# Per-head projections as float32 in column halves, and the second head's turned rows copied by two engines

## The chip, the cores and the metric

The kernel runs on one core of a Trainium2 chip. The time is the device time of one execution in microseconds (us). Every number of the trace comes from one profiled execution on that core. The engines are named as the profile names them: PE is TensorE (PEld its weight loads), DVE is VectorE, ACT is ScalarE, POOL is GpSimd, SP issues most of the DMAs.

## The reference, cut to what matters

The program is a network of two layers on x of 2 batches of 1024 rows of 128. Layer 0 is one causal attention head and a mixture of experts. Layer 1, in which nearly all of the time goes, is attention with 16 heads of 64 columns and a bias by relative position, and then a feed-forward part with 8 low-rank experts.

```python
h = _layernorm(x) * (1 + ca) + sa
q, k, v = shape(h @ Wq), shape(h @ Wk), shape(h @ Wv)      # 16 heads of 64
scores = einsum('bhqd,bhkd->bhqk', q, k)
weights = softmax(scores + position_bias)
context = einsum('bhqk,bhkd->bhqd', weights, v)
x = x + ga * (context.reshape(B, S, H * Dk) @ Wo)
```

The products that the change touches are h @ Wq, h @ Wk and h @ Wv of this layer.

## The kernel before, in words

Heads go in 8 pairs, and a pair and a batch make a unit: 16 units (UNITS). A unit has 8 tiles of 128 query rows, so there are 128 tiles (TILES), and the attention is one software pipeline of slots n, one tile per slot. All engines run the slots in the same order, each in its own function, and semaphores tie them; no scheduler moves anything, so the order of the code is the order on the engine.

In slot n PE runs `pe_slot`: the scores of tile n+2 (`pe_scores`: three passes of high and low parts in fp32r, two heads in row halves of the array, 12 matmuls of 512 columns into the banks SC), the turning of head 0's weights of tile n (`pe_turn`: 16 transposes into the two banks PT[0] and PT[1]), one chunk of the next unit's projections into the bank MI where the slot has one (`pe_chunk`), half of the weights-times-values product of the tile pair before (`pe_values`, the heads in column halves of the array, into CX), the turning of head 1 into the same two banks PT, and, in even slots, the product with Wo (`pe_wo`).

A unit has six chunks: q and k in two halves each of 512 columns, v in two halves of four row tiles. They stand in slots 0, 1, 2, 3, 5 and 7 of the unit before. So every odd slot holds a chunk, and slots 4 and 6 hold none. The last unit has no chunks to make, and unit 0's chunks are made before the slots begin. A q or k chunk is three fp32r matmuls of 128 x 128 weights against 512 columns: high h by high w, low h by high w, high h by low w. For this ACT writes `h_high` behind each `hT`, DVE or POOL writes `h_low`, and POOL writes `wsplit` (`pool_split`) for every head pair. A v chunk is four float32 matmuls of 128 columns.

The two banks PT are one buffer for both heads. Head 0's turned rows are copied by ACT (`act_turned`), head 1's by DVE (`dve_turned`), each 1024 columns out of both banks. `pe_turn(n, 1)` waits for ACT's copy of the same slot (`ptA_out`), and `pe_turn(n, 0)` for DVE's copy of the slot before (`ptB_out`).

In slot n ACT runs, in this order: head 0's copy, the exponential of tile n+2's head 0, the chunk's copy out of MI, the exponential of head 1, and in odd slots the copy of the context (`ctxs`). DVE runs, in this order: in odd slots the two products out of `pe_wo` (`dve_wo`), the bias and row maximum of tile n+2 for both heads (`dve_biased`), and head 1's copy.

Before the slots, a quarter of the rows at a time is gathered from the experts, normalised (`norm_scaled` on DVE), turned on PE (`turn_rows`, line 1160) and written to `hT` by ACT (line 753). The last two quarters, batch 1, come between slots 0 and 1.

Of the kernel before, what the change touches and what calls it, by code (L numbers as in the profile page):

```python
# [14 lines left out]
F32 = mybir.dt.float32  # L15
# [7 lines left out]
P = 128  # L23
# [41 lines left out]
def build(nc, rel_hot, L0_attn_x, L0_attn_Wq, L0_attn_bq, L0_attn_Wk, L0_attn_bk, L0_attn_Wv, L0_attn_bv,  # L65
# [4 lines left out]
    with ExitStack() as ctx:  # L70
# [18 lines left out]
        h_high = sb("h_high", [P, N], F32R)  # L89
        h_low = sb("h_low", [P, N], F32R)  # L90
        h_parts = (h_high, h_low)
# [25 lines left out]
        wsplit = sb("wsplit", [P, 2, 2, 2, P], F32R)  # L117
# [39 lines left out]
        lowrank = [part(h_high, 0, 512), part(h_high, 512, 512)]  # L157
        masked = h_low[:, :].rearrange("p (j a n) -> p j a n", j=2, a=2)
# [123 lines left out]
        def act_chunk(act, u, c):  # L282

            kind, q = chunk_of(u, c)
            act.wait_ge(ev("proj_full"), 6 * u + c + 1)
# [41 lines left out]
        def pe_chunk(pe, u, c):  # L327
# [3 lines left out]
            if c == 0 and b == 0:  # L331
                pe.wait_ge(ev("w_split"), p + 1)
# [5 lines left out]
            else:  # L338
                n = (u - 1) * TB + slots_of(u)[c]
                if u == 1 and c == 0:  # L340
                    pe.wait_ge(ev("low_out"), 4)
# [35 lines left out]
        def pe_turn(pe, n, hd):  # L377
# [17 lines left out]
        def pe_values(pe, g, half):  # L395

            if half == 0:
                pe.wait_ge(ev("ptA_out"), 2 * g + 2)
                pe.wait_ge(ev("ptB_out"), 2 * g + 2)
                pe.wait_ge(ev("ctx_out"), g)  # L400
# [74 lines left out]

        def act_exp(act, n, hd):
# [8 lines left out]
        def act_slot(act, n):  # L485
# [11 lines left out]
            if n + 2 < TILES:  # L497
                act_exp(act, n + 2, 1)
            if n >= 3 and n % 2 == 1:
# [19 lines left out]
        def dve_turned(dve, n):  # L519
# [4 lines left out]
            dve.tensor_copy(turned_out(n, 1), turned_in(1)).then_inc(ev("ptB_out"), 1)  # L524
# [37 lines left out]
        def pool_split(pool, p):  # L562

# [837 lines left out]
```

## Time and profile before

| | us |
|---|---|
| median of 3 runs | 1039.62 (1037.82 to 1041.65) |
| the profiled execution's own time | 1039.06 |
| its span, first to last instruction | 1037.3 |
| PE busy | 934.1 (90%) |
| DVE busy | 668.4 (64%) |
| ACT busy | 590.0 (57%) |
| POOL busy | 281.7 (27%) |

The profiled execution lies 1.8 us over its span and 0.6 us under the median. The slots run from about 224 us to 946 us of the span. In front of them stand layer 0 and the gathering of the experts' rows, behind them the last feed-forward part. A timeline row gives the start, the length from the first start to the last end of a merged group, the engine, the line, what is written from what, and the number of instructions. A float32 matmul of the program is two matmul instructions in the trace, each with its weight load. The length of a matmul reaches beyond the start of the next, since they are pipelined, so the distance between the starts of two groups tells what a group takes from PE.

### The profile page before, as it was taken

The page shows a single profiled execution, that of the slowest core. Times are in us where ns is not written, and L with a number is a line of the kernel's source. Part 1 is how long each engine was busy: PE and PEld are TensorE (multiplying, and loading weights), DVE is VectorE, ACT ScalarE, POOL GpSimd, SP SyncE. Part 2 cuts the span into 40 slices and gives each one's busy share as a digit, 9 for nine tenths or more (in the row PEclk, how much of TensorE's full clock was granted, in tenths as well). Part 3 has the DMA queues.
Part 4 walks back from the last instruction along what each step waited for, and adds up shares of the span by engine and source line. Part 5 has one row for each costly group of instructions (what it writes and reads, how often), then busy time and mean ns, then how long its engine had stood idle before and what let it go on. Part 6 is the DMA issues. An engine that isn't in the chain of part 4 may idle for free. (4 is left out here: it accounts for less than half of the span.)

```text
span 1037.3 us, 24542 instructions
## 1 busy us (share of the span) xinstructions
PE 934.1 (90%) x9958; PEld 687.5 (66%) x9958; DVE 668.4 (64%) x1352; ACT 590.0 (57%) x980; POOL 281.7 (27%) x332
## 2 busy tenths in 40 slices
PE   7888349457999999999999999999999999996897
PEld 6467338345777777677777767777777776774786
DVE  6277401285767777677677777667777776774665
ACT  2533113236666766766766676676667667672343
POOL 1100540332341422324233142333414233112300
PEclk9999769767999999999999999999999999999999
DMA  8301231100002002000200200110020010000000
GB/s 260 109 1 73 94 89 31 56 23 1 2 2 85 2 2 86 2 2 2 85 3 1 86 2 2 42 46 3 2 85 2 2 37 3 1 3 2 1 21 21
DMA packets 27124, 35.43 MB, mean 34 GB/s; under 512 B 6042, under 2 KB 21716, under 8 KB 26836
## 3 DMA queue, kind: packets, MB, share of 16 engines
q1 hardware_dynamic: 25988, 31.76, 9.2%
q0 software_dynamic: 1024, 2.10, 0.7%
q8 instruction: 80, 1.31, 0.5%
q14 instruction: 32, 0.26, 0.1%
HBM read 28.48 MB, written 5.37 MB: 33 GB/s over the span
## 5 line engine op out<-in xcount | busy, mean ns | idle before, releaser
L516 DVE CUSTOM_DVE_ANT_0 soft<-SC,strips 128x1024 f32<-128x1024 f32 x256 | 303.2, 1221 | 21.1 <-PE SC L372 21.1
L482 ACT ACTIVATE soft<-soft,nmax 128x1024 f32<-128x1024 f32 x256 | 294.0, 1149 | 2.8 <-DVE nmax L516 2.8
L524 DVE COPY PTs<-PT 128x1024 f32<-128x1024 f32 x128 | 156.8, 1225 | 186.0 <-PE PT L390 186.0
L474 ACT COPY PTs<-PT 128x1024 f32<-128x1024 f32 x128 | 129.8, 1014 | 223.9 <-PE PT L390 223.9
L406 PE MATMUL CX<-PTs,V 128*64 128x256 f32 x2048 | 250.7, 387 | 5.7 <-DVE wo_out L533 4.3
L372 PE MATMUL SC<-qk 64*128 64x512 f32 x1536 | 212.4, 409 | 10.4 <-DVE nmax L516 7.0
L390 PEld LDWEIGHTS PT<-ident,soft 64*128 64x128 f32 x4096 | 155.6, 139 | 86.5 <-issue 75.6
L406 PEld LDWEIGHTS CX<-PTs,V 128*64 128x64 f32 x2048 | 136.7, 137 | 89.7 <-issue 24.6
L390 PE MATMUL PT<-ident,soft 64*128 64x64 f32 x4096 | 180.1, 228 | 3.7 <-DVE PTs L524 2.4
L372 PEld LDWEIGHTS SC<-qk 64*128 64x128 f32 x1536 | 137.1, 188 | 35.5 <-issue 4.7
L557 POOL TENSOR_TENSOR x<-x,wo_out 128x256 f32<-128x256 f32 x64 | 47.1, 736 | 259.3 <-DVE wo_out L533 259.3
L322 POOL CAST qk<-raw_qk 128x512 fp32r<-128x512 f32 x60 | 36.8, 614 | 225.1 <-ACT raw_qk L298 225.1
L324 POOL TENSOR_TENSOR qk<-raw_qk,qk 128x512 fp32r<-128x512 f32 x60 | 77.5, 1292 | 4.8
L354 PE MATMUL MI<-h_high,wsplit 128*128 128x512 f32 x122 | 55.6, 455 | 2.9 <-DVE h_low L1045 2.9
L482 ACT ACTIVATION_READ_ACCUMULATOR soft<-soft,nmax 128x1 f32 x256 | 49.3, 193 | 0.0
L806 ACT ACTIVATE probsT<-SC,cols 128x384 f32<-128x384 f32 x32 | 18.6, 581 | 53.9 <-PE SC L1280 52.4
L560 POOL TENSOR_TENSOR x<-x,wo_out 128x256 f32<-128x256 f32 x64 | 47.5, 742 | 5.0
L425 PE MATMUL CX<-wog,ctxs 64*128 64x128 f32 x256 | 42.4, 286 | 0.5 <-ACT ctxs L505 0.5
L425 PE MATMUL MI<-wog,ctxs 64*128 64x128 f32 x256 | 42.4, 286 | 0.0
L1130 PE MATMUL SC<-ident 128*128 128x128 f32 x110 | 17.4, 316 | 24.9 <-DMA slots_in<-probsT,arena 24.9
L841 ACT ACTIVATE probsT<-SC,cols 128x512 f32<-128x512 f32 x32 | 21.9, 690 | 28.2 <-PE SC L1363 28.1
L298 ACT ACTIVATE raw_qk<-MI 128x512 f32<-128x512 f32 x60 | 35.2, 587 | 0.0
(235 smaller groups left out, 1041.4 us busy)
## 6 DMA issues: line engine op xcount, KB each, us to landing
strips<-bias_vec SPq DMA_DIRECT2D x8, 1920.0 KB, 7.1
arena<-in_L_ffn_w SPq DMA_DIRECT2D x1, 2048.0 KB, 10.4
slots_in<-arena SPq DMA_DIRECT2D x1, 1536.0 KB, 9.1
arena<-slots_in SPq DMA_DIRECT2D x8, 192.0 KB, 3.9
slots_out<-arena SPq DMA_DIRECT2D x8, 192.0 KB, 2.0
x<-in_L_attn_x SPq DMA_DIRECT2D x2, 512.0 KB, 4.6
out<-x SPq DMA_DIRECT2D x4, 256.0 KB, 2.3
arena<-in_L_wmod SPq DMA_DIRECT2D x2, 384.0 KB, 5.6
```

The lines of the kernel that those rows point to most:

```text
L324: pool.tensor_tensor(qk[u % 2][:, k + 1, at], raw_qk[:, c % 2, :], qk[u % 2][:, k, at].bitcast(F32), ALU.subtract).then_inc(ev("low_out"), 1)
L354: ins = pe.matmul(bank, wsplit[:, p % 2, wp, "qk".index(kind), :], rhs, start=(n == 0), stop=(n == 2))
L372: ins = pe.matmul(SC[hd][:, k * CK:(k + 1) * CK], qk[u % 2][mine, qp, i * P:(i + 1) * P], qk[u % 2][mine, kp, k * CK:(k + 1) * CK], start= ...
L390: ins = pe.transpose(PT[r][:, t * DK:(t + 1) * DK], soft[mine, n % RING, hd, t * P:(t + 1) * P], ident[mine, mine])
L406: ins = pe.matmul(CX[hd * DK:(hd + 1) * DK, 0:2 * P], V1[:, vb, t, hd * DK:(hd + 1) * DK], PTs[:, g % 2, hd, t, :], start=(t == 0), stop=( ...
L425: ins = pe.matmul(dst, ctxs[mine, g % 4, t * P:(t + 1) * P], wog[mine, u % B, u // B, :], start=(hd == 1 or (g == GROUPS - 1 and t == 0)), ...
L474: act.copy(turned_out(n, 0), turned_in(0)).then_inc(ev("ptA_out"), 1)
L482: act.activation(soft[:, n % RING, hd, :], soft[:, n % RING, hd, :], ACT.Exp, bias=nmax[:, j:j + 1], scale=-1.0, accum_out=rsum[:, hd, n % ...
L516: dve.tensor_tensor_reduce(soft[:, n % RING, hd, :], SC[hd][:, :], strips[:, u // B % 2, hd, i * P:i * P + S], 1.0, 3.4e38, ALU.add, ALU.m ...
L524: dve.tensor_copy(turned_out(n, 1), turned_in(1)).then_inc(ev("ptB_out"), 1)
L557: pool.tensor_tensor(x[:, t0:t0 + 2, :], x[:, t0:t0 + 2, :], wo_out[:, g % 2, 1, :, :], ALU.add).then_inc(ev("x_half"), 1)
L560: pool.tensor_tensor(x[:, t0:t0 + 2, :], x[:, t0:t0 + 2, :], wo_out[:, g % 2, 0, :, :], ALU.add).then_inc(ev("x_added"), 1)
```

## The change

1. A q or k chunk is now two float32 matmuls, one for each head of the pair: the weights are 64 columns of `wpair`, the output the partitions 0 to 63 or 64 to 127 of the bank, the moving operand the 512 columns of `hT` for both. A v chunk is eight float32 matmuls, two for each row tile: 64 columns of `hT` as weights, `wpair` (128 columns) moving.
2. `h_high`, `h_low` and `wsplit`, with all instructions that write them, are gone. PE waits for `hT_ready` and `ld_pair` in their place.
3. Head 1's turned rows are copied in two parts: DVE takes PT[0], ACT takes PT[1] (`act_turned_half`), 512 columns each. ACT does its part behind the exponential of head 1 and ahead of the copy of the context. `pe_turn(n, 0)` and `pe_values` wait for both.
4. On DVE slot -1 comes ahead of the scaling of batch 1's rows (`norm_rows(2, (1,))`), which stood between slots -2 and -1.
5. `proj_full` counts two for each chunk, and the buffers `lowrank` and `masked` of the last part are buffers of their own.

```diff
@@ pe_chunk
-            if kind == "v":
-                for t in range(4):
-                    ins = pe.matmul(bank[:, t * P:(t + 1) * P], hT[:, b * S + (4 * q + t) * P:b * S + (4 * q + t + 1) * P], wpair[:, p % 2, 2, :], start=True, stop=True)
-            else:
-
-                for n, (hp, wp) in enumerate(((0, 0), (1, 0), (0, 1))):
-                    rhs = h_parts[hp][:, b * S + q * CK:b * S + (q + 1) * CK]
-                    if kind == "q":
-                        rhs = bass.AP(h_parts[hp], b * S + S - 1 - q * CK, [[N, P], [-1, CK]])
-                    ins = pe.matmul(bank, wsplit[:, p % 2, wp, "qk".index(kind), :], rhs, start=(n == 0), stop=(n == 2))
-            ins.then_inc(ev("proj_full"), 1)
+            rhs = hT[:, b * S + q * CK:b * S + (q + 1) * CK]
+            if kind == "q":
+                rhs = bass.AP(hT, b * S + S - 1 - q * CK, [[N, P], [-1, CK]])
+            for t in range(4 if kind == "v" else 1):
+                for r in range(2):
+                    mine = slice(r * DK, (r + 1) * DK)
+                    if kind == "v":
+                        at = b * S + (4 * q + t) * P + r * DK
+                        ins = pe.matmul(bank[mine, t * P:(t + 1) * P], hT[:, at:at + DK], wpair[:, p % 2, 2, :], start=True, stop=True)
+                    else:
+                        ins = pe.matmul(bank[mine, :], wpair[:, p % 2, "qk".index(kind), mine], rhs, start=True, stop=True)
+                    if t == 3 or kind != "v":
+                        ins.then_inc(ev("proj_full"), 1)
@@ pe_turn, head 0 (and the same wait in pe_values)
                     pe.wait_ge(ev("ptB_out"), n)
+                    pe.wait_ge(ev("ptB_half"), n)
@@ new, called in act_slot behind the second act_exp
+        def act_turned_half(act, n):
+
+            act.wait_ge(ev("ptB_full"), 2 * n + 2)
+            if n >= 4:
+                act.wait_ge(ev("pv_done"), n // 2 - 1)
+            act.copy(turned_out(n, 1)[:, 1, :, :], PT[1][:, :].rearrange("p (t q) -> p t q", t=TB)).then_inc(ev("ptB_half"), 1)
@@ dve_turned
-            dve.tensor_copy(turned_out(n, 1), turned_in(1)).then_inc(ev("ptB_out"), 1)
+            dve.tensor_copy(turned_out(n, 1)[:, 0, :, :], PT[0][:, :].rearrange("p (t q) -> p t q", t=TB)).then_inc(ev("ptB_out"), 1)
@@ norm_out on ACT (the subtraction into h_low goes on DVE and POOL, too)
-                    if n == 2:
-
-                        act.wait_ge(ev("hT_ready"), 4 * n + k + 1)
-                        at = slice(reversed_block(k) * 512, (reversed_block(k) + 1) * 512)
-                        act.copy(h_high[:, at], hT[:, at]).then_inc(ev("h_high"), 1)
@@ vector
             dve_slot(dve, -2)
+            dve_slot(dve, -1)
             norm_rows(2, (1,))
-            for n in range(-1, TILES + 4):
+            for n in range(TILES + 4):
@@ tensor
-            pe.wait_ge(ev("h_split"), 1)
+            pe.wait_ge(ev("hT_ready"), 9)
...
-            pe.wait_ge(ev("h_split"), 4)
```

On PE, in an odd slot and the start of the even one behind it, there stood before (L354 is the chunk, L406 the values, L390 the transposes, L372 the scores):

```order
L354 MATMUL MI<-h_high,wsplit 128x512
L406 MATMUL CX<-PTs,V 64x256 [waits s_woA_out]
L406 MATMUL CX<-PTs,V 64x256 x7
L390 MATMUL PT<-ident,soft 128x64 [waits s_ptA_out,s_exp_done]
L390 MATMUL PT<-ident,soft 128x64 x15
L372 MATMUL SC<-qk 128x512 [waits s_nmax_done]
L372 MATMUL SC<-qk 128x512 x11
L390 MATMUL PT<-ident,soft 128x64 [waits s_ptB_out,s_exp_done]
L390 MATMUL PT<-ident,soft 128x64 x15
L354 MATMUL MI<-h_high,wsplit 128x512 [waits s_woB_out,s_high_out]
L354 MATMUL MI<-h_low,wsplit 128x512
L354 MATMUL MI<-h_high,wsplit 128x512
```

In the changed kernel the same place reads (L352 is the chunk, L407 the values, L371 the scores):

```order
L352 MATMUL MI<-hT,wpair 64x512
L407 MATMUL CX<-PTs,V 64x256 [waits s_woA_out]
L407 MATMUL CX<-PTs,V 64x256 x7
L390 MATMUL PT<-ident,soft 128x64 [waits s_ptA_out,s_exp_done]
L390 MATMUL PT<-ident,soft 128x64 x15
L371 MATMUL SC<-qk 128x512 [waits s_nmax_done]
L371 MATMUL SC<-qk 128x512 x11
L390 MATMUL PT<-ident,soft 128x64 [waits s_ptB_half,s_ptB_out,s_exp_done]
L390 MATMUL PT<-ident,soft 128x64 x15
L352 MATMUL MI<-hT,wpair 64x512 [waits s_woB_out,s_high_out]
L352 MATMUL MI<-hT,wpair 64x512
```

The order of the groups is the same. The chunk writes 64 partitions at a time, as the values behind it do, and the first transposes of the even slot wait for one semaphore more.

On ACT, the end of an odd slot and the start of the next, before (L482 is the exponential, L505 the context, L474 head 0's copy, L298 the chunk):

```order
L298 ACTIVATE raw_qk<-MI 128x512 [waits s_low_out,s_proj_full]
L482 ACTIVATE soft,rsum<-soft,nmax 128x1024 [waits s_rinv_done,s_nmax_done]
L505 COPY ctxs<-CX 128x256 [waits s_woB_full,s_woA_full,s_pv_done]
L474 COPY PTs<-PT 128x2x8x64 [waits s_pv_done,s_ptA_full]
L482 ACTIVATE soft,rsum<-soft,nmax 128x1024 [waits s_rinv_done,s_nmax_done]
```

And in the changed kernel (L490 is the exponential, L482 now the new half copy, L515 the context, L285 a v chunk, L475 head 0's copy):

```order
L285 COPY V1<-MI 128x512 [waits s_pv_done,s_proj_full]
L490 ACTIVATE soft,rsum<-soft,nmax 128x1024 [waits s_rinv_done,s_nmax_done]
L482 COPY PTs<-PT 128x8x64 [waits s_pv_done,s_ptB_full]
L515 COPY ctxs<-CX 128x256 [waits s_woB_full,s_woA_full,s_pv_done]
L475 COPY PTs<-PT 128x2x8x64 [waits s_pv_done,s_ptA_full]
```

One copy more stands behind the second exponential, ahead of the context's copy.

On DVE, at the first slots, before (L516 is the bias and maximum, L884 to L890 the scaling of batch 1's rows):

```order
L516 ISA soft,nmax<-SC,strips 128x1024 [waits s_strips0,s_scores]
L516 ISA nmax 128x1
L884 RECIPROCAL st<-st 128x8 [waits s_root_ready,s_var_ready]
L885 TENSOR_TENSOR st<-st 128x8 [waits s_dve_step]
...
L890 TENSOR_SCALAR probs<-x,mv,st 128x128 x7
L516 ISA soft,nmax<-SC,strips 128x1024 [waits s_scores]
L516 ISA nmax 128x1
```

And in the changed kernel (L526 is the bias and maximum, L873 to L879 the scaling):

```order
L526 ISA soft,nmax<-SC,strips 128x1024 [waits s_scores]
L526 ISA nmax 128x1
L526 ISA soft,nmax<-SC,strips 128x1024 [waits s_scores]
L526 ISA nmax 128x1
L873 RECIPROCAL st<-st 128x8 [waits s_root_ready,s_var_ready]
L874 TENSOR_TENSOR st<-st 128x8 [waits s_dve_step]
```

The bias and maximum of tile 1, which waits for that tile's scores, has moved ahead of the scaling.

## Rows read from the trace of the kernel before

**Rows 1.** The page: span, PE's busy time, PE's granted clock in 40 slices.

```profile
span 1037.3 us, 24542 instructions
PE 934.1 (90%) x9958; PEld 687.5 (66%) x9958; DVE 668.4 (64%) x1352; ACT 590.0 (57%) x980; POOL 281.7 (27%) x332
PEclk9999769767999999999999999999999999999999
```

**Rows 2.** The timeline, 500 to 512 us: an odd slot, then an even one.

```profile
500.57 1.23 PEld L372 LDWEIGHTS SC<-qk 64*128 64x128 f32 x12
501.84 0.74 PEld L390 LDWEIGHTS PT<-ident,soft 64*128 64x128 f32 x16
502.65 0.97 PEld L347 LDWEIGHTS MI<-wpair,hT 128*128 128x128 f32 x8
502.79 1.01 ACT L474 COPY PTs<-PT 128x1024 f32<-128x1024 f32 x1 [1.65 <-PE PT L390]
503.74 1.49 PEld L406 LDWEIGHTS CX<-PTs,V 128*64 128x64 f32 x16
505.31 1.16 ACT L482 ACTIVATE soft<-soft,nmax 128x1024 f32<-128x1024 f32 x1
505.62 0.58 PEld L390 LDWEIGHTS PT<-ident,soft 64*128 64x128 f32 x16 [0.39 <-issue]
506.11 1.24 PEld L372 LDWEIGHTS SC<-qk 64*128 64x128 f32 x12
506.40 1.23 DVE L524 COPY PTs<-PT 128x1024 f32<-128x1024 f32 x1 [1.76 <-PE PT L390]
506.46 0.37 ACT L505 COPY ctxs<-CX 128x256 f32<-128x256 f32 x1
507.75 0.61 PEld L390 LDWEIGHTS PT<-ident,soft 64*128 64x128 f32 x16 [0.40 <-issue]
508.42 0.19 PEld L354 LDWEIGHTS MI<-h_high,wsplit 128*128 128x128 f32 x1
508.53 1.02 ACT L474 COPY PTs<-PT 128x1024 f32<-128x1024 f32 x1 [1.71 <-PE PT L390]
509.32 1.49 PEld L406 LDWEIGHTS CX<-PTs,V 128*64 128x64 f32 x16 [0.37 <-issue]
```

**Rows 3.** The timeline, the first us of the values, asked in short windows.

```profile
509.32 0.44 PE L406 MATMUL CX<-PTs,V 128*64 128x256 f32 x2
509.32 0.14 PEld L406 LDWEIGHTS CX<-PTs,V 128*64 128x64 f32 x2 [0.37 <-issue]
509.59 0.82 PE L406 MATMUL CX<-PTs,V 128*64 128x256 f32 x6
```

**Rows 4.** Groups by line and shape: copies of 512 columns out of a bank.

```profile
L941 DVE COPY probsT<-PT 128x512 f32<-128x512 f32 x1 | 0.7, 692 | 0.9 <-PE PT L1214 0.9
L289 ACT COPY V<-MI 128x512 f32<-128x512 f32 x28 | 16.1, 575 | 0.0
```

**Rows 5.** The timeline by engine, 209 to 247 us: hT, its parts, PE behind them.

```profile
210.17 0.78 ACT L753 ACTIVATE hT<-SC,modc 128x512 f32<-128x512 f32 x1 [3.51 <-PE SC L1160]
212.98 0.80 PE L354 MATMUL PT<-h_high,wsplit 128*128 128x512 f32 x1 [2.84 <-DVE h_low L1045]
217.88 0.78 ACT L753 ACTIVATE hT<-SC,modc 128x512 f32<-128x512 f32 x1
220.72 0.80 PE L354 MATMUL MI<-h_high,wsplit 128*128 128x512 f32 x1 [2.92 <-DVE h_low L1045]
222.17 0.63 PE L354 MATMUL PT<-h_high,wsplit 128*128 128x512 f32 x1
222.59 0.63 PE L354 MATMUL PT<-h_low,wsplit 128*128 128x512 f32 x1
231.89 2.14 DVE L890 TENSOR_SCALAR probs<-x,mv,st 128x128 f32<-128x128 f32 x8
```

**Rows 6.** The same view: where PE waits for the last of h_low.

```profile
246.93 2.93 PE L372 MATMUL SC<-qk 64*128 64x512 f32 x12 [3.33 <-POOL h_low L710]
```

More of the change, by code:

```diff
@@ L88, in build @@
         x = sb("x", [P, NT, D])
-        h_high = sb("h_high", [P, N], F32R)
-        h_low = sb("h_low", [P, N], F32R)
-        h_parts = (h_high, h_low)
+        masked = sb("masked", [P, 2, 2, 512], F32R)
         with nc.sbuf_tensor("arena", [P, 8 * N], F32) as arena:
@@ L116, in build @@
         wpair = sb("wpair", [P, 2, 3, P])
-        wsplit = sb("wsplit", [P, 2, 2, 2, P], F32R)
+        lowrank = sb("lowrank", [P, 2, 512], F32R)
         strips = sb("strips", [P, 2, 2, STRIP])
@@ L284, in act_chunk @@
             kind, q = chunk_of(u, c)
-            act.wait_ge(ev("proj_full"), 6 * u + c + 1)
+            act.wait_ge(ev("proj_full"), 2 * (6 * u + c + 1))
             if kind == "v":
@@ L331, in pe_chunk @@
             if c == 0 and b == 0:
-                pe.wait_ge(ev("w_split"), p + 1)
+                pe.wait_ge(ev("ld_pair"), 48 * p + 48)
+            if c == 0 and u == 1:
+                pe.wait_ge(ev("hT_ready"), 12)
+                pe.wait_ge(ev("low_out"), 4)
             bank = chunk_bank(u, c)
@@ L399, in pe_values @@
                 pe.wait_ge(ev("ptB_out"), 2 * g + 2)
+                pe.wait_ge(ev("ptB_half"), 2 * g + 2)
                 pe.wait_ge(ev("ctx_out"), g)
@@ L498, in act_slot @@
                 act_exp(act, n + 2, 1)
+            if 0 <= n < TILES:
+                act_turned_half(act, n)
             if n >= 3 and n % 2 == 1:
@@ L575, in pool_slot @@
                 pool_chunk(pool, a, c)
-            if n % (B * TB) == 4 and n // (B * TB) + 1 < PAIRS:
-                pool_split(pool, n // (B * TB) + 1)
         block = ctx.enter_context(nc.Block())
@@ L631, in _ @@
                 if p >= 2:
-                    sp.wait_ge(ev("proj_full"), 12 * (p - 1))
+                    sp.wait_ge(ev("proj_full"), 24 * (p - 1))
                 load_weights(sp, p)
@@ L705, in _ @@
                                         bass.IndirectOffsetOnAxis(ap=slot_g[:, t:t + 1], axis=0)).then_inc(ev("gathered%d" % (t // 4)), 16)
-            for k in range(2, 4):
-                pool.wait_ge(ev("h_high"), k + 1)
-                at = slice(reversed_block(k) * 512, (reversed_block(k) + 1) * 512)
-                pool.tensor_tensor(h_low[:, at], hT[:, at], h_high[:, at].bitcast(F32), ALU.subtract).then_inc(ev("h_split"), 1)
             for n in range(-2, TILES + 4):
@@ L755, in norm_out @@
                                    bias=modc[:, layer, m, k // 2:k // 2 + 1]).then_inc(ev("hT_ready"), 1)
-                    if n == 2:
-                        act.wait_ge(ev("hT_ready"), 4 * n + k + 1)
-                        at = slice(reversed_block(k) * 512, (reversed_block(k) + 1) * 512)
-                        act.copy(h_high[:, at], hT[:, at]).then_inc(ev("h_high"), 1)
             norm_roots(0)
@@ L833, in _ @@
                     act.wait_ge(ev("masked"), 2 * k)
-                act.copy(lowrank[0], MI[:, :]).then_inc(ev("low_ready"), 1)
+                act.copy(lowrank[:, 0, :], MI[:, :]).then_inc(ev("low_ready"), 1)
                 for j in range(2):
@@ L1039, in quarter_rows @@
                 norm_scaled(quarter(q))
-            def split_h(k):
-                at = slice(reversed_block(k) * 512, (reversed_block(k) + 1) * 512)
-                dve.wait_ge(ev("h_high"), k + 1)
-                tt(h_low[:, at], hT[:, at], h_high[:, at].bitcast(F32), ALU.subtract).then_inc(ev("h_split"), 1)
             gathered(0)
@@ L1300, in _ @@
             turn_rows(2, 1)
-            pe.wait_ge(ev("h_split"), 2)
+            pe.wait_ge(ev("hT_ready"), 10)
             pe_chunk(pe, 0, 3)
```

19 lines of the change are left out of this document (3 added, 16 removed).

## The prediction

> **What bounds the kernel now.** I read the page first: PE is busy 90% of a span of 1037.3 us, and its granted clock is at the full level, 2.4 GHz, in every slice of the slots [rows 1]. So the 128 slots are PE's, and what counts is how far apart the starts of its groups lie. The timeline of one odd and one even slot shows that [rows 2]. The reader is to look at the distance between weight loads of successive groups on PEld. From the scores at 500.57 to the transposes at 501.84 it is 1.27 us, that is 12 matmuls in 6 pairs of row halves, 0.21 us for 512 columns in one pass. From the scores at 506.11 to the transposes at 507.75 it is 1.64 us for the same work. The difference is a wait: DVE's copy of head 1's turned rows starts at 506.40, takes 1.23 and ends at 507.63, and PE goes on 0.12 us later. At 501.84 there was no wait, since the product with Wo stood in between. The next group begins 0.81 us behind the unhindered transposes (502.65 - 501.84) and 0.67 us behind the delayed ones (508.42 - 507.75), since there the first weights are loaded while the scores still stream. Scores and transposes together take 2.08 us without the wait and 2.31 with it: the wait costs 0.23 us, not 0.37. It stands at the start of every even slot.
>
> The second thing to see is what a chunk takes: 0.90 us for q or k (508.42 to 509.32), of which three passes of 512 columns stream for 3 x 0.21 = 0.64, and 1.09 us for v (502.65 to 503.74). The values behind take 1.88 us (503.74 to 505.62), of which 8 pairs of column halves stream 1.71. A chunk thus carries about 0.25 us that is no streaming, and PEld is idle 0.37 us ahead of the values behind it [rows 2].
>
> **The waits of the even slots.** Split copies of 512 columns: DVE's costs 0.69 us and ACT's 0.58 us, both from rows of copies of that size out of a bank [rows 4]; DVE's price was 1.23 for 1024. DVE would end at 506.40 + 0.69 = 507.09. ACT has to end its exponential first (505.31 + 1.16 = 506.47), so it ends at 507.05, and with 0.12 for the release PE may go on at 507.17 to 507.21. PE is through with the scores at 506.11 + 1.27 = 507.38. The wait is gone, with 0.2 us to spare. If PE comes 0.23 us earlier because of a cheaper v chunk (below), ACT's half is as late as PE, at most 0.06 us later, and such a delay is paid by the load of the first weights, as the 0.81 against 0.67 shows. Odd slots have the Wo product in between (about 0.45 us more), so nothing waits there. ACT's added 0.58 us stands in idle time: it is idle 1.71 us ahead of the next copy at 508.53, behind the context's copy (506.46 + 0.37) [rows 2]. Queued behind the new copy are the context's copy, which PE's Wo product needs only a slot later, and head 0's copy, still over 1 us away. Were that cover gone, each of the 128 slots could cost up to 0.58. Even slots 2 to 124 have scores ahead of the transposes: 62 x 0.23 = 14.3 us. Behind them come two slots and the last values without scores to hide any of the copy. There the shorter copy shows by 1.23 - 0.69 = 0.5 us each: 1.5 us. **Term 1: -15.8 us.** What is late next is PE itself.
>
> **The chunks.** A float32 product streams twice the columns in each of its two instructions. The values show it: 256 columns, 8 products of each head half, and the starts of the pairs lie 0.21 us apart, since six matmuls that begin at 509.59 span 0.82 us, and a last one takes 0.38 to 0.44 of that [rows 3]. The two halves start together (two matmuls span 0.44 us, two loads 0.14) [rows 3], and 8 x 0.21 = 1.71 leaves no room for a stagger in the 1.88. So a new q or k chunk has 2 pairs of 512 columns, 2 x 0.43 = 0.85 us, and a new v chunk 8 pairs of 128 columns, 8 x 0.107 = 0.85 us. As to what is no streaming, the chunk now has the form of the values, 128*64, and runs into them: I take one start (0.06: 509.32 to 509.59 less 0.21) and one end for both, so that chunk and values take 0.85 + 1.88 = 2.73 us. Before it was 0.90 + 1.88 = 2.78 and 1.09 + 1.88 = 2.97. That is -0.04 for q and k, and -0.24 for v. There are 15 units with 4 and 2 of them in the slots: 60 x -0.04 + 30 x -0.24 = -9.6. The nearest bound on the other side is that the 0.24 remains at the border of chunk and values: q and k +0.19, v 0.0, in sum +11.4. I take the first end, because in the rows a border is paid where the form of the matmuls changes (0.17 us of the 1.88 behind the values) and groups of one form follow without loss (1.27 us for six pairs). **Term 2: -9.6 us.**
>
> The Trainium skill (TensorEngine Tiling, Key Properties) says that a change of the tiling mode drains TensorE. The PEld idle of 0.37 us between chunk and values agrees with it. Without that rule the sum would have +11.4 in place of -9.6.
>
> **The start.** PE waited for h_low. The first h was written at 210.17 + 0.78 = 210.95 and PE began at 212.98; the second at 218.66, and PE began at 220.72 [rows 5]. Each gives 2.0 us. In this stretch PE runs at the lower level, 1.2 GHz: the starts of 512-column passes lie 0.42 apart (222.17, 222.59). A q or k chunk of float32 is there 1.71 us against 1.28, +0.43, for four of them 1.7. Net -2.3. Later PE waits 3.33 us at 246.93 for POOL's h_low [rows 6], which goes whole: next is the turning of batch 1's rows, that ends at this wait's start. Against this stands the moved scaling on DVE. Its 8 instructions of 2.14 us and five small ones, about 3.1 us together, ran while PE made the scores of tile 1; now they come behind that tile's maximum and delay the next. I count that as +0.5, because the scores of tile 2 can meanwhile run; the bounds are 0 and +3.1. **Term 3: -2.3 - 3.3 + 0.5 = -5.1 us** (-2.5 to -7.5; the clock may also rise a little sooner).
>
> POOL loses 1.1 us for each head pair and was never waited for in the slots; the separate buffers at the end change no instruction. Both count nothing.
>
> **The sum.** 1039.06 - 15.8 - 9.6 - 5.1 = 1008.6 us, for the profiled execution; the median lies 0.6 higher, so 1009 us.
>
> **The rivals.** (a) *The wait stays*, because ACT's half comes late. ACT's chain in an odd slot is copy, exponential, chunk, exponential, half copy, from 502.79 to 507.05 without a hole, and PE's from 502.65 to 507.15 in the new kernel. The slack is thin, which speaks for it; that a delay under 0.14 us costs nothing speaks against. If it all stayed, term 1 falls to 1.5: 1023 us.
> (b) *The border stays*: chunk and values don't run together. 1009 + 21 = 1030 us. (a) and (b) together: 1044 us.
> (c) *Weights lie open.* Should loads of one column half not run beside matmuls of the other, each pair of loads adds its 0.14 us: 2 in a q or k chunk, 8 in a v chunk, 60 x 0.28 + 30 x 1.12 = +50, so 1059 us. The values speak against: with it their 8 pairs would take 2.8 us, and they take 1.88 [rows 2, 3]. The Trainium skill (TensorE: Matmul & The Clock Gate, Part 3) gives such a rule: weight loads overlap running matmuls only where the row group differs, and column halves share theirs. The trace does not agree with it here.
> (d) *The halves run one after another*, the slower end. Both halves of a q or k chunk read the same 512 columns, and write one bank. The values write one bank too, but read different data, so only this differs. Each chunk would stream 0.85 us more: 90 x 0.85 = +77, 1086 us. The change is slower than the kernel before from the point where a chunk costs 0.33 us more than I take (30 / 90).
> (e) *More than forecast*: the clock rises earlier at the start, and the last slots gain more: below 1001 us.
>
> **How the numbers follow.** Forecast 0.64, (a) 0.10, (b) 0.07, (a) and (b) 0.05, (c) 0.03, (d) 0.05, (e) 0.06. The bounds of terms 1 to 3 give the forecast 1002 to 1017. To hold 8 in 10 I go over (a), up to 1027, and down to 1001. A measurement of this kernel can tell 0.5%, about 5 us. Only (c) and (d) are slower than 1045, 0.08; (a) and (b) together give no change, 0.05; all else is faster, 0.87.
>
> **What would show it.** Right: the distance from scores to transposes is 1.27 us in even slots too; a q or k chunk begins 0.85 us ahead of its values, a v chunk as well; the idle of PEld ahead of the values is gone; an even and an odd slot with q and v chunks lie nearer by 0.5 us together; PE's first scores of tile 3 come at about 241.8, not 246.93. Wrong on term 1: transposes that start 0.1 us behind ACT's half copy, with the 1.27 not reached. Wrong on term 2: chunk to values 1.0 us or more, or pairs of the chunk whose starts lie 0.4 us apart within a pair. Wrong on term 3: a long idle of PE ahead of tile 2's scores or of the turning of batch 1's rows.

## The result and the profile after

The changed kernel takes 1010.09 us (median of 6 runs, 1007.98 to 1014.62), beside 1039.67 us (1037.82 to 1042.87) for the kernel before. The ratio is 0.9718, with an interval of 0.9691 to 0.9745. It is faster, and lies 1 us above the forecast of 1009. The profiled execution took 1007.98 us, over a span of 1006.1 us. From here on, "after" is the changed kernel.

The first lines of its page answer to [rows 1]. ACT and PE's clock stand with them, and so do the groups of the two half copies:

```profile
span 1006.1 us, 25473 instructions
PE 910.8 (91%) x10278; PEld 674.7 (67%) x10278; DVE 601.5 (60%) x1350; ACT 648.6 (64%) x1104; POOL 268.3 (27%) x314
PEclk9999769978999999999999999999999999997999
...
L534 DVE COPY PTs<-PT 128x512 f32<-128x512 f32 x128 | 88.5, 692 | 165.2 <-PE PT L390 165.1
L390 PE MATMUL PT<-ident,soft 64*128 64x64 f32 x4096 | 176.2, 226 | 3.7 <-ACT PTs L482 2.1
L482 ACT COPY PTs<-PT 128x512 f32<-128x512 f32 x128 | 74.0, 578 | 3.1 <-PE PT L390 3.1
```

The reader is to see that PE still bounds the kernel (91%), that DVE has 67 us less work and ACT 59 us more, and that the two copies cost 692 and 578 ns each, the prices of [rows 4]. The row of the transposes can't tell whether the wait of the even slots is gone. It puts 2.1 us to ACT's half (L482), in the whole execution, and the same row of the kernel before put 2.4 us to DVE's copy, where 62 waits of 0.23 us stood:

```profile
L390 PE MATMUL PT<-ident,soft 64*128 64x64 f32 x4096 | 180.1, 228 | 3.7 <-DVE PTs L524 2.4
```

The distances between the starts of groups do tell it.

The timeline of an odd slot and the start of the even one behind it answers to [rows 2]. L350 is a v chunk, L352 a q or k chunk, L407 the values, L390 the transposes, L371 the scores, L490 the exponential:

```profile
484.08 0.85 PEld L350 LDWEIGHTS MI<-wpair,hT 128*64 128x64 f32 x16
484.90 1.55 PEld L407 LDWEIGHTS CX<-PTs,V 128*64 128x64 f32 x16
486.74 1.16 ACT L490 ACTIVATE soft<-soft,nmax 128x1024 f32<-128x1024 f32 x1
486.83 0.57 PEld L390 LDWEIGHTS PT<-ident,soft 64*128 64x128 f32 x16 [0.39 <-issue]
487.32 1.24 PEld L371 LDWEIGHTS SC<-qk 64*128 64x128 f32 x12
487.61 0.69 DVE L534 COPY PTs<-PT 128x512 f32<-128x512 f32 x1 [1.54 <-PE PT L390]
487.88 0.58 ACT L482 COPY PTs<-PT 128x512 f32<-128x512 f32 x1
488.60 0.75 PEld L390 LDWEIGHTS PT<-ident,soft 64*128 64x128 f32 x16
489.42 0.20 PEld L352 LDWEIGHTS MI<-hT,wpair 128*64 128x64 f32 x4
489.90 0.15 PEld L407 LDWEIGHTS CX<-PTs,V 128*64 128x64 f32 x2 [0.28 <-issue]
490.33 1.44 PEld L407 LDWEIGHTS CX<-PTs,V 128*64 128x64 f32 x14 [0.28 <-issue]
```

From scores to transposes it is now 488.60 - 487.32 = 1.28 us in an even slot, where it was 1.64. DVE's half ends at 488.30 and ACT's at 488.46, and PE goes on at 488.60, 0.14 behind the later one. In the trace of before the transposes followed DVE's copy by 0.12. So ACT is just in time, with next to nothing to spare.

The v chunk begins 0.82 us ahead of its values, and chunk and values together take 2.75 (484.08 to 486.83). For a q or k chunk the same sum is 2.74 on the mean. But here the values load their first weights 0.48 behind the chunk's start, not 0.85: the two loads (x2 at 489.90) run while the chunk still streams, and then PEld is idle 0.28 until the values' matmuls begin at 490.33, 0.91 behind the chunk's first.

**Where the 31.2 us of span went.** I cut both executions at three marks: the first turning of gathered rows on PE, the first values and the last values.

| stretch | before | after | difference |
|---|---|---|---|
| up to the first turning | 209.05 | 206.78 | -2.3 |
| first turning to first values | 46.55 | 38.31 | -8.2 |
| first to last values (the slots) | 695.7 | 673.1 | -22.6 |
| last values to the end | 86.0 | 87.9 | +1.9 |

Of these the slots are the steadiest. Another execution of the same program (e7_after_again) gave 672.8, and so did two variants (e5, which leaves the slots alone, and e9, which moves one copy in them to another engine). The first stretch scatters: 206.5 to 211.9 in the twelve traces of this case.

The slots by their parts, as the mean distance between the starts of weight loads over some 55 places each, 30 for v:

| | before | after |
|---|---|---|
| even slot: scores to transposes, to the next group | 1.637 + 0.675 | 1.285 + 0.813 |
| q or k chunk and values | 2.773 | 2.737 |
| v chunk and values | 2.966 | 2.750 |

That is -0.214 for each of 62 even slots, -0.036 for each of 60 q and k chunks and -0.216 for each of 30 v chunks: -13.3 - 2.2 - 6.5 = -22.0. The waits at the last two transposes shrank too, from 2.16 and 2.11 us between the starts of neighbouring groups to 1.58 and 1.79, together 0.9. That makes -22.9, 0.3 us more than the stretch lost. In two of the 62 even slots, both in the last unit, the transposes still start 1.55 us behind the scores; more on them below.

### The profile page after: what moved, and what is told of

It is laid out like the page before. It is cut to its first block and busy times, and to the rows that moved or that the text cites. A ratio compares the mean times of both kernels' runs of the same rounds, so it can differ in the third digit from the quotient of the medians.

```text
span 1006.1 us, 25473 instructions
## 1 busy us (share of the span) xinstructions
PE 910.8 (91%) x10278; PEld 674.7 (67%) x10278; DVE 601.5 (60%) x1350; ACT 648.6 (64%) x1104; POOL 268.3 (27%) x314
## 5 line engine op out<-in xcount | busy, mean ns | idle before, releaser
L526 DVE CUSTOM_DVE_ANT_0 soft<-SC,strips 128x1024 f32<-128x1024 f32 x256 | 303.3, 1222 | 80.2 <-PE SC L371 80.1
L490 ACT ACTIVATE soft<-soft,nmax 128x1024 f32<-128x1024 f32 x256 | 294.1, 1150 | 2.8 <-DVE nmax L526 2.8
L407 PE MATMUL CX<-PTs,V 128*64 128x256 f32 x2048 | 246.5, 383 | 5.1 <-DVE wo_out L543 4.1
L371 PE MATMUL SC<-qk 64*128 64x512 f32 x1536 | 212.0, 408 | 7.3 <-DVE nmax L526 6.5
L475 ACT COPY PTs<-PT 128x1024 f32<-128x1024 f32 x128 | 129.6, 1012 | 136.6 <-PE PT L390 136.6
L407 PEld LDWEIGHTS CX<-PTs,V 128*64 128x64 f32 x2048 | 143.6, 138 | 97.8 <-issue 36.5
L390 PEld LDWEIGHTS PT<-ident,soft 64*128 64x128 f32 x4096 | 158.9, 139 | 69.7 <-issue 31.2
L534 DVE COPY PTs<-PT 128x512 f32<-128x512 f32 x128 | 88.5, 692 | 165.2 <-PE PT L390 165.1
L390 PE MATMUL PT<-ident,soft 64*128 64x64 f32 x4096 | 176.2, 226 | 3.7 <-ACT PTs L482 2.1
L371 PEld LDWEIGHTS SC<-qk 64*128 64x128 f32 x1536 | 137.5, 188 | 32.1 <-issue 4.7
L482 ACT COPY PTs<-PT 128x512 f32<-128x512 f32 x128 | 74.0, 578 | 3.1 <-PE PT L390 3.1
L352 PE MATMUL MI<-hT,wpair 128*64 128x512 f32 x244 | 65.8, 618 | 1.0 <-ACT hT L747 1.0
L795 ACT ACTIVATE probsT<-SC,cols 128x384 f32<-128x384 f32 x32 | 18.6, 580 | 53.1 <-PE SC L1262 51.6
L490 ACT ACTIVATION_READ_ACCUMULATOR soft<-soft,nmax 128x1 f32 x256 | 49.3, 193 | 0.0
```

The costliest lines, as they stand in the source:

```text
L352: ins = pe.matmul(bank[mine, :], wpair[:, p % 2, "qk".index(kind), mine], rhs, start=True, stop=True)
L371: ins = pe.matmul(SC[hd][:, k * CK:(k + 1) * CK], qk[u % 2][mine, qp, i * P:(i + 1) * P], qk[u % 2][mine, kp, k * CK:(k + 1) * CK], start= ...
L390: ins = pe.transpose(PT[r][:, t * DK:(t + 1) * DK], soft[mine, n % RING, hd, t * P:(t + 1) * P], ident[mine, mine])
L407: ins = pe.matmul(CX[hd * DK:(hd + 1) * DK, 0:2 * P], V1[:, vb, t, hd * DK:(hd + 1) * DK], PTs[:, g % 2, hd, t, :], start=(t == 0), stop=( ...
L475: act.copy(turned_out(n, 0), turned_in(0)).then_inc(ev("ptA_out"), 1)
L482: act.copy(turned_out(n, 1)[:, 1, :, :], PT[1][:, :].rearrange("p (t q) -> p t q", t=TB)).then_inc(ev("ptB_half"), 1)
```

## The experiments

Each kernel was compared with the kernel before on its own chip. The table gives the ratio of the times, and beside it the stretch from first to last values of the profiled execution, since the start and the first stretch scatter by a few us.

| | ratio (interval) | slots, us |
|---|---|---|
| after | 0.9718 (0.9691 to 0.9745) | 673.1 |
| e1_split_only | 0.9845 (0.9789 to 0.9901) | 682.1 |
| e2_proj_only | 0.9825 (0.9773 to 0.9876) | 687.4 |
| e3_whole_f32 | 0.9888 (0.9826 to 0.9951) | 691.2 |
| e4_half_last | 0.9801 (0.9739 to 0.9862) | 680.5 |
| e5_rows_first | 0.9664 (0.9634 to 0.9695) | 672.8 |
| e6_bf16_halves | 0.9555 (0.9518 to 0.9592) | 657.3 |
| e7_after_again | 0.9692 (0.9650 to 0.9734) | 672.8 |
| e8_bf16_v_dve | 0.9554 (0.9526 to 0.9582) | 655.4 |
| e9_v_dve | 0.9723 (0.9686 to 0.9759) | 672.8 |
| e10_bf16_again | 0.9589 (0.9541 to 0.9637) | 657.2 |

The kernel before has 695.7 us of slots.

### One part alone: e1_split_only and e2_proj_only

e1 is the kernel before with the divided copy and nothing else.

```diff
@@ dve_turned, and act_turned_half behind act_exp(act, n + 2, 1)
-            dve.tensor_copy(turned_out(n, 1), turned_in(1)).then_inc(ev("ptB_out"), 1)
+            dve.tensor_copy(turned_out(n, 1)[:, 0, :, :], PT[0]...).then_inc(ev("ptB_out"), 1)
+            act.copy(turned_out(n, 1)[:, 1, :, :], PT[1]...).then_inc(ev("ptB_half"), 1)
@@ pe_turn, pe_values
+                    pe.wait_ge(ev("ptB_half"), n)
...
```

> The kernel before with the divided copy alone: DVE copies PT[0], ACT copies PT[1], the projections stay three fp32r passes of 128 columns, and h_high, h_low and wsplit stay. Theory (the wait of the even slots was for DVE's copy and is worth 0.21 to 0.23 us each): scores to transposes 1.27 us in even slots, 62 x 0.22 plus about 1.2 at the end, so 15 us less than the kernel before: 1025 us. Rival (the gain needs the cheaper chunks, because ACT's half is late): the 1.27 isn't reached, time 1033 to 1040 us.

e2 is the changed kernel with DVE's undivided copy.

```diff
@@ dve_turned
-            dve.tensor_copy(turned_out(n, 1)[:, 0, :, :], PT[0]...).then_inc(ev("ptB_out"), 1)
+            dve.tensor_copy(turned_out(n, 1), turned_in(1)).then_inc(ev("ptB_out"), 1)
@@ pe_turn, pe_values, act_slot
-                    pe.wait_ge(ev("ptB_half"), n)
...
-                act_turned_half(act, n)
```

> The changed kernel with the copy undivided again: DVE copies all 1024 columns, ACT none of head 1. Theory (the terms add up): scores to transposes is 1.64 us again in even slots, 1.23 us of copy behind head 1's transposes, and 14 to 15 us come back: 1025 us. Rival (with shorter chunks DVE's copy is early enough, or another wait had been the cause): 1010 to 1014 us.

e1 took 1030.95 us beside 1046.77, that is 15.8 less where 15 was expected, and e2 took 1028.26. The chip was slower than the first one, on which the kernel before takes 1039.67, so the expected times are met in their differences and not as they stand. Each part alone is faster than the kernel before, since both intervals lie below 1. The slots of e1 are 13.6 us shorter than before. The distance from scores to transposes in even slots is 1.28, with 1.55 in the same two of the last unit. With the next group it is 2.10 on the mean, as in after: 62 x (2.31 - 2.10) = 13, and the end of the slots gives the same 0.9 as in after. In e2 the distance is 1.636 as before, its chunks measure as in after, and its slots are 8.3 shorter than before and 14.3 longer than after's. The two parts sum to -21.9 us, and the whole change has -22.6. So within 0.7 us the parts neither help nor hinder each other. Their terms had -15.8 and -9.6.

### What the column halves are worth: e3_whole_f32

The changed kernel, with one float32 product of 128 columns of weights in place of the pair of halves, for v as for q and k.

```diff
@@ pe_chunk
-                for r in range(2):
-                    mine = slice(r * DK, (r + 1) * DK)
...
-                        ins = pe.matmul(bank[mine, :], wpair[:, p % 2, "qk".index(kind), mine], rhs, start=True, stop=True)
...
+                    ins = pe.matmul(bank, wpair[:, p % 2, "qk".index(kind), :], rhs, start=True, stop=True)
```

> The changed kernel with the same float32 products over all 128 columns at once: one product per q or k chunk, four per v chunk, in place of two and eight halves. The streamed columns take the same 0.85 us. Theory (the chunk's gain is the border that falls away when it has the form of the values): chunk and values take 2.97 us instead of 2.74, for q and k as for v, so 90 x 0.23 = 21 us more: 1031 us. Rival (the form is of no matter, the gain is that of float32 against three passes): 1010 us.

The slots are 18.1 us longer than after's, where 21 was expected. In PEld's timeline a q or k chunk and its values stand so:

```profile
506.50 0.30 PEld L350 LDWEIGHTS MI<-hT,wpair 128*128 128x128 f32 x2
507.56 0.41 PEld L404 LDWEIGHTS CX<-PTs,V 128*64 128x64 f32 x6 [0.76 <-issue]
```

The values' first weights come 1.06 behind the chunk's start and not 0.48, and PEld is idle 0.76 ahead of them. The values' matmuls start with these weights, 1.06 behind the chunk's first, where it was 0.91. Chunk and values take 2.935 on the mean for q and k (+0.20) and 2.97 for v (+0.22): 60 x 0.20 + 30 x 0.22 = 18.6. The form of the chunk, which the prediction bounded at 0.24, is thus worth 0.20 to 0.22 us. Not all of it is the border. Of the 0.20, some 0.05 lies inside the chunk, whose two products start 0.53 us apart (506.51, 507.04) where the halves' pairs start 0.48 apart (489.42, 489.90). The other 0.15 is lost from the chunk's last product to the end of the values. The run also shows what float32 is worth without the column halves. Against e1, which differs in the slots by its chunks and their parts on POOL and has the three fp32r passes, e3's slots are 9.1 us longer: whole float32 products lose, and the halves turn that into a gain of 9.0.

### How thin ACT's slack is: e4_half_last

The changed kernel, with ACT's half behind the copy of the context.

```diff
@@ act_slot
-            if 0 <= n < TILES:
-                act_turned_half(act, n)
...
                 act.copy(ctxs[:, g % 4, :], CX[:, 0:2 * P]).then_inc(ev("ctx_out"), 1)
+            if 0 <= n < TILES:
+                act_turned_half(act, n)
```

> The changed kernel with ACT's half copy behind the copy of the context instead of ahead of it, which moves it by 0.39 us in odd slots alone. Theory (the slack of ACT's half in odd slots is about 0.14 us or less beyond the end of the scores): PE's first transposes of an even slot come 0.37 us later than now, 0.14 of it is made good by the early weight load, 62 x 0.23 = 14 us more: 1024 us. Rival (ACT has 0.4 us or more to spare): 1010 us.

ACT and PEld at the start of an even slot:

```profile
504.84 1.24 PEld L371 LDWEIGHTS SC<-qk 64*128 64x128 f32 x12
505.40 0.37 ACT L513 COPY ctxs<-CX 128x256 f32<-128x256 f32 x1
505.65 0.61 ACT L482 COPY PTs<-PT 128x512 f32<-128x512 f32 x1
506.37 0.61 PEld L390 LDWEIGHTS PT<-ident,soft 64*128 64x128 f32 x16 [0.29 <-issue]
```

ACT's half starts 0.25 us behind the context's copy, not the 0.37 of its duration, since the two overlap in the records. It ends at 506.26, and PE goes on 0.11 later, 1.53 behind the scores. The next group then follows in 0.675 and not 0.813, so each even slot loses 1.529 + 0.675 - 1.285 - 0.813 = 0.11 us: 62 x 0.11 = 6.8. The slots are 7.4 us longer than after's, half of the 14 us expected, since the expectation took the whole 0.37 as delay. Of the delay of 0.25 us the next group gives back 0.14, as it did in the kernel before (0.67 behind delayed transposes, 0.81 behind the others).

### The moved scaling of the rows: e5_rows_first and e7_after_again

e5 is the changed kernel with batch 1's scaling back between slots -2 and -1 on DVE; e7 is the changed kernel itself.

```diff
@@ vector
             dve_slot(dve, -2)
-            dve_slot(dve, -1)
             norm_rows(2, (1,))
-            for n in range(TILES + 4):
+            for n in range(-1, TILES + 4):
```

> The changed kernel with the scaling of batch 1's rows back between DVE's slots -2 and -1, as in the kernel before. Theory (the move costs a little, since the 3.1 us of scaling lose the cover of tile 1's scores): the bias of tile 2 starts about 0.9 us sooner behind the bias of tile 1, and the first scores of tile 3 come up to 0.9 us sooner, time 1009 against 1010 us, within the noise. Rival (the move is what brought the start its extra 2.6 us): the first scores of tile 3 come 2 us or more later, 1012 us.

> The changed kernel itself, on the same chip as the two before it, as their measure: a ratio of 0.972 to the kernel before, as on the other chip. First values 38 us behind the first turning of gathered rows, scores to transposes 1.28 us in even slots.

e5 took 1007.85 us (1006.37 to 1008.82) and e7 1009.79 (1008.04 to 1014.19). The ratios' intervals overlap, and no difference is shown. In the traces tile 2's first bias comes 10.1 us behind tile 0's in e5 and 10.9 in after and in e7, so the move costs 0.8 us at that place. But PE's first scores of tile 3 come 30.79 us behind the first turning in e5 and 30.17 in after, since in e5 the turning of batch 1's rows ran at the lower clock. In e7 they come 28.76 behind. The move itself is worth less than the start scatters.

### A cheaper chunk: e6_bf16_halves and e10_bf16_again

From unit 2 on, a chunk is three passes of bf16 parts in column halves: high h by high w, low h by high w, high h by low w. The product of low by low is left out, and the parts have bf16's precision. POOL makes the parts of h in slots 3 to 6 and those of w once for each head pair. Units 0 and 1 stay float32.

```diff
@@ pe_chunk, from unit 2 on
+                for n, (hp, wp) in enumerate(((0, 0), (1, 0), (0, 1))):
+                    for r in range(2):
...
+                            rhs = h_parts[hp][:, b * S + q * CK:b * S + (q + 1) * CK]
+                            ins = pe.matmul(bank[mine, :], wsplit[:, p % 2, wp, "qk".index(kind), mine], rhs, start=(n == 0), stop=(n == 2))
@@ new
+            pool.tensor_copy(h_high[:, at], hT[:, at]).then_inc(ev("h_high"), 1)
...
+            pool.tensor_tensor(h_low[:, at], hT[:, at], h_high[:, at], ALU.subtract).then_inc(ev("h_split"), 1)
```

> The changed kernel, but from unit 2 on a chunk is three bf16 passes of high and low parts in column halves (POOL makes the parts), in place of float32 halves. A q or k chunk then streams 3 x 0.21 = 0.64 us instead of 0.85, still in the form of the values. Theory (PE is the bound and the streamed columns are the price): chunk and values 2.52 us, 0.21 less. In odd slots PE then runs 0.2 us into ACT's half copy, which costs 0.09 of it. A v chunk has 24 products of 128 columns and gains between 0 and 0.21. In sum 8 to 13 us less: 997 to 1002 us. Rival (ACT's half copy is the bound now): transposes of even slots start 0.1 us behind its end, and what the chunk saves is waited off: 1007 to 1010 us.

> The bf16 kernel again, on the same chip as the two before it, as their measure: 0.956 of the kernel before, 1.50 us from scores to transposes in even slots.

The bf16 kernel took 995.05 us beside 1042.15, and 998.5 beside 1042.52 on another chip: 0.9555 and 0.9589. Both are below the ratio of the change, and this version beats both kernels. Its slots are 15.8 us shorter than after's, where 8 to 13 was expected. A q or k chunk with its values takes 2.494 (-0.243) and a v chunk 2.52 (-0.23), for 56 and 28 of them 20.0 us. The rest goes back into a wait. ACT and PEld of e6 at the start of an even slot:

```profile
503.23 1.24 PEld L396 LDWEIGHTS SC<-qk 64*128 64x128 f32 x12
504.04 0.58 ACT L507 COPY PTs<-PT 128x512 f32<-128x512 f32 x1
504.74 0.61 PEld L415 LDWEIGHTS PT<-ident,soft 64*128 64x128 f32 x16 [0.27 <-issue]
505.41 1.49 PEld L432 LDWEIGHTS CX<-PTs,V 128*64 128x64 f32 x16
```

ACT's half ends at 504.62 and PE goes on at 504.74, 1.51 behind the scores. On the mean it is 1.50 + 0.675 where after has 1.285 + 0.813: +0.08 for each of about 56 even slots, 4.5 us. That is the prediction's rival (a), at the next step: PE became 0.24 us faster in the odd slot, and ACT's chain did not.

### Is it ACT's chain: e8_bf16_v_dve and e9_v_dve

To tell that from another cause, the v chunk's copy out of MI goes from ACT to DVE, with bf16 chunks (e8) and in the changed kernel (e9). It takes 0.57 us off ACT's chain ahead of the half copy in the odd slots that hold a v chunk, and nothing in those with q or k.

```diff
@@ act_slot
             if what == "chunk":
-                act_chunk(act, a, c)
+                if chunk_of(a, c)[0] != "v":
+                    act_chunk(act, a, c)
@@ dve_slot, behind dve_biased(dve, n + 2, 1)
+            if what == "chunk" and chunk_of(a, c)[0] == "v":
...
+                dve.tensor_copy(V1[:, a % 2, 4 * q:4 * q + 4, :]..., chunk_bank(a, c)).then_inc(ev("high_out"), 1)
```

> The bf16 kernel with the copy of the v chunks out of MI moved from ACT to DVE, behind its second bias. ACT's chain in slots 5 and 7 gets 0.47 us shorter. Theory (in the bf16 kernel ACT's half copy ends 0.23 us behind PE's scores and costs 0.08 us in each odd slot): the slots behind a v chunk go from 1.50 to 1.28 us from scores to transposes, those behind a q or k chunk stay at 1.50; 28 x 0.08 = 2 us less than the bf16 kernel. Rival (DVE's copy of PT[0] is the late one, or DVE gets the bound by the 0.69 us added to it): 1.50 stays or grows, and time with it.

> The changed kernel with the same move of the v chunks' copy to DVE. Theory (in the changed kernel ACT's half is just in time, so nothing waits for it): no change, 1.27 to 1.28 us from scores to transposes as before, the same time within 2 us. Rival (ACT is the bound of the changed kernel): 2 us or more less.

In e8 the even slots behind a v chunk have 1.28 again (28 places), and those behind q or k still 1.50. One of each in e8's timeline, behind a v chunk first:

```profile
521.86 1.24 PEld L396 LDWEIGHTS SC<-qk 64*128 64x128 f32 x12
522.15 0.69 DVE L560 COPY PTs<-PT 128x512 f32<-128x512 f32 x1 [0.71 <-PE PT L415]
522.18 0.57 ACT L507 COPY PTs<-PT 128x512 f32<-128x512 f32 x1
523.14 0.74 PEld L415 LDWEIGHTS PT<-ident,soft 64*128 64x128 f32 x16
```

```profile
501.08 1.24 PEld L396 LDWEIGHTS SC<-qk 64*128 64x128 f32 x12
501.37 0.69 DVE L560 COPY PTs<-PT 128x512 f32<-128x512 f32 x1 [1.29 <-PE PT L415]
501.90 0.58 ACT L507 COPY PTs<-PT 128x512 f32<-128x512 f32 x1
502.59 0.61 PEld L415 LDWEIGHTS PT<-ident,soft 64*128 64x128 f32 x16 [0.27 <-issue]
```

In the first ACT's half ends 0.39 us ahead of PE's transposes (some 0.11 of it is the release), in the second it ends at 502.48 and PE follows 0.11 later. DVE's half had ended at 502.06. The slots are 1.8 us shorter than e10's, which agrees with 28 x (0.22 - 0.14) = 2.2; by their ratios e8 and e10 can't be told apart. In e9 the distance is 1.281 and the slots take 672.8 us, as in after: there the copy was not late, and nothing was to be had. So it is the length of ACT's chain that PE waits for in e6. Behind a v chunk the experiment shows it. Behind q and k it is read from the 0.11 us between the end of ACT's half and PE's start.

## Why the prediction was right

**Term 1, the waits of the even slots: right.** Forecast 0.23 us each, measured 0.214; with the end of the slots (1.5 forecast, 0.9 measured) -14.2 against -15.8. The reasoning that a wait costs less than it lasts, because the next weights are loaded under it, was needed: by the distance from scores to transposes alone one would have counted 0.35. e4 shows the same from the other side. The slack was put at 0.2 us, to fall to nothing behind a v chunk, and next to nothing is what the trace shows. But the 0.2 was read from an odd slot with a v chunk, and the prediction gave none for q and k. In e1, which has the old chunks, ACT's half ends 0.35 us ahead of the transposes behind a v chunk and only 0.17 ahead behind q or k, of which 0.11 is the release. In after both have 0.12 to 0.15. So the term had less room than it said, and held. Rival (a) came in at two of the 62 even slots of after, behind odd slots of the last unit in which PE turns weights of the last part in place of a chunk, in less time. In the first of the two ACT's half ends at 883.12 and the transposes start at 883.24, 1.55 behind the scores, at a cost of 0.12 us. It came in full view in e6.

**Term 2, the chunks: right in sum, wrong in one sign.** Forecast -0.04 and -0.24, measured -0.036 and -0.216, -8.7 us against -9.6. The choice between the two ends rested on the row in which a border is paid where the form changes, and e3 shows that this is so: with the form of before the border stays, 0.20 to 0.22 us for each chunk. What I named as the sign of it was wrong for q and k. I said that the chunk would begin 0.85 us ahead of its values and that PEld's idle would be gone. In the trace the first loads of the values come 0.48 behind the chunk's start, and an idle of 0.28 follows. The loads are early, not late: two weights are loaded under the chunk's last products, and the next come with the values' own matmuls. These start 0.91 behind the chunk's, the 0.06 + 0.85 of the sum. The sign belonged on PE's rows and not on PEld's. Of rivals (c) and (d) nothing is seen. Chunk and values would have taken 2.74 + 0.28 or more by (c) and 3.6 by (d). The Trainium skill (TensorE: Matmul & The Clock Gate, Part 3) lists that weight loads overlap running matmuls only where the row group differs. The paragraph above that list also lets them go ahead into a background weight buffer. Here the values' loads, of the same row group, begin 0.43 us ahead of their matmuls, under those of the chunk, so the trace agrees with the paragraph and not with the list on which rival (c) drew. The Trainium skill (TensorEngine Tiling, Key Properties) says that changing the tiling mode drains TensorE. The run e3 agrees with it: with the change of form chunk and values cost 0.20 to 0.22 us more.

**Term 3, the start: right in what happens, too small.** Forecast -5.1 (bounds -2.5 to -7.5), measured -8.2, outside these bounds. The rows, in the order of time, of PE, ACT and DVE (L1142 turns rows, L747 writes hT, L352 and L350 are unit 0's chunks, L371 the scores, L526 the bias, L879 the scaling):

```profile
206.78 1.09 PE L1142 MATMUL SC<-ident,probs 128*128 128x128 f32 x4 [15.23 <-DVE probs L879]
207.91 0.78 ACT L747 ACTIVATE hT<-SC,modc 128x512 f32<-128x512 f32 x1 [3.51 <-PE SC L1142]
208.74 3.69 PE L352 MATMUL PT<-hT,wpair 128*64 128x512 f32 x8 [0.87 <-ACT hT L747]
212.21 1.86 PE L350 MATMUL CX<-wpair,hT 128*64 128x128 f32 x16
215.53 1.08 PE L352 MATMUL MI<-hT,wpair 128*64 128x512 f32 x4 [0.87 <-ACT hT L747]
216.44 1.03 PE L352 MATMUL PT<-hT,wpair 128*64 128x512 f32 x4
222.38 1.22 DVE L526 CUSTOM_DVE_ANT_0 soft<-SC,strips 128x1024 f32<-128x1024 f32 x1
231.22 2.14 DVE L879 TENSOR_SCALAR probs<-x,mv,st 128x128 f32<-128x128 f32 x8
233.27 1.22 DVE L526 CUSTOM_DVE_ANT_0 soft<-SC,strips 128x1024 f32<-128x1024 f32 x1
235.92 0.66 PE L1142 MATMUL CX<-ident,probs 128*128 128x128 f32 x4
236.42 0.60 PE L1142 MATMUL MI<-ident,probs 128*128 128x128 f32 x4
236.95 1.66 PE L371 MATMUL SC<-qk 64*128 64x512 f32 x12
```

And of before, the same rows of DVE and PE (L516 is the bias, L1160 turns rows):

```profile
228.52 1.23 DVE L516 CUSTOM_DVE_ANT_0 soft<-SC,strips 128x1024 f32<-128x1024 f32 x1
238.53 1.23 DVE L516 CUSTOM_DVE_ANT_0 soft<-SC,strips 128x1024 f32<-128x1024 f32 x1 [2.18 <-PE SC L372]
241.62 1.12 PE L1160 MATMUL CX<-ident,probs 128*128 128x128 f32 x4
242.53 1.06 PE L1160 MATMUL MI<-ident,probs 128*128 128x128 f32 x4
```

The waits for h_low are gone, as forecast: the first chunk follows hT by 0.05 us (207.91 + 0.78 = 208.69, as against 2.0). Tile 0's first bias moved from 19.47 us behind the first turning to 15.60, which is -3.9 where the term had -2.3. The cause is the clock. The step counted all four q and k chunks at 1.2 GHz, +0.43 each. The third and fourth stand 0.91 apart (215.53, 216.44), which is the full level: there a float32 chunk is not dearer than the three passes at the lower level, 1.28, at which the kernel before made the same chunks, but cheaper. So two chunks got dearer and two got cheaper by about as much, and nearly all of the 4.0 us of the two waits was won. The last part of the term was 3.3 us for POOL's h_low, and that wait is gone whole. The scaling in its new place cost 0.9 us (-3.9 became -3.0 at tile 2's bias), where 0.5 was taken. Then batch 1's rows were turned in 0.50 us a quarter (235.92, 236.42, 236.95), where before it was 0.91. PE's first scores of tile 3 came at 236.95; I had named 241.8, which left out the 2.3 us by which everything in front came sooner as well; the rest is mostly the clock's, 1.6 at the chunks and 0.8 at the turning. That the waits for h_low cost what they lasted was not tested alone: it is read from these rows.

This size is one of single executions. Before stands with one trace. The changed start has 38.3, 39.2, 38.3 and 36.9 us from first turning to first values in after, e5, e6 and e7, and 42.3 to 42.6 in e3, e4, e8, e9 and e10. In the latter the engines stop for some us; of e9, on ACT:

```profile
217.70 0.59 ACT L285 COPY V<-CX 128x512 f32<-128x512 f32 x1 [3.78 <-remote]
```

Nothing in the trace names what ends it. The kernel before's trace has no such stop, so -8.2 compares like with like; with a stop in the changed kernel it would be -4. It seems to go with the chip: e2 to e4 of one chip and e8 to e10 of another have it, and e5 to e7 of a third have none. The run e1 is of the first of these chips and has the start of the kernel before. It has no such stop, but takes 48.97 us there and not 46.55, so on that chip the changed start gains 6.6 us in e3 and e4, and 4.1 in e2, stop included. What the stop is stays open.

**What the sum left out.** The stretch ahead of the first turning was 2.3 us shorter and the one behind the last values 1.9 longer. Neither is touched in a way that explains it. The first stretch scatters by 5 us. The last one lies between 85.8 and 90.0 in the twelve traces, and it goes with the granted clock in it: 85.8 to 87.0 us at a mean of 0.96 (before, e3, e6, e8, e10), 87.4 at 0.95 (e4), 87.8 to 88.0 at 0.93 (after, e2, e5, e7, e9), 90.0 at 0.90 (e1). In after this is the slice at 7 tenths, the fourth digit from the end in the PEclk row above. Why the clock fell there for longer isn't shown. The two nearly cancel, and so do the shortfall of terms 1 and 2 (2.5 us) and the excess of term 3 (3.1 us). The forecast's closeness, 1 us, is thus better than its parts: they were off by 1 to 3 us each. Two statements of the prediction were not sound. The range of 1002 to 1017 is said to follow from the bounds of the three terms, but those given, of term 3 alone, make it 1007 to 1012. And full clock "in every slice of the slots" does not hold for the first slots, where the ninth and tenth digit of [rows 1] are 6 and 7 tenths; term 3 itself counts the lower level there.

## What to carry to other kernels

Where two groups of matmuls follow one another on PE, give them the same array shape: the form was worth 0.20 to 0.22 us here, about as much as bf16 passes saved inside a chunk in e6 (0.23 to 0.24). Judge a wait by the distance to the group behind it and not by its own length, since the next weights load under it; and before taking work off PE, measure how far ahead of need the engine that has to release it ends, because a few tenths of a us off PE make that engine the next bound. At a start where PE's clock changes, price each group at the level that it will meet in the new order, and not at the one it met in the old: two chunks here moved from the lower level to the full one.

## What the hardware showed unexpectedly

- Weight loads of the values ran ahead under the matmuls of the chunk, with both groups in column halves, but only the first two: they came 0.48 us behind a q or k chunk's start, and PEld then had a pause of 0.28.
- Three bf16 passes in column halves ran at the rate of fp32r passes, 0.21 to 0.24 us for each pair of 512 columns (e8: L377 at 503.26, 503.50 and 503.72), so that such a chunk streams for 0.64 us where float32 streams for 0.85.
- Two copies that follow each other on ACT cost less than their durations say: the one behind the other started 0.25 us after it, at a duration of 0.37.
- Six traces of two chips show a stop at about 212 to 222 us, with idle time of up to 4.5 us on ACT and a releaser that is not in the trace; e1, of one of these chips, and the traces of the other chips show none.
- The stretch behind the slots, with the same 442 matmuls on PE in all twelve traces, took 85.8 to 87.0 us at a mean granted clock of 0.96 and 90.0 at 0.90.
